# A sparse-mask mixture of experts on one core: the next batch's routing placed among a batch's last three tiles

## What is computed

```
adj  = side (column) * cond (row) * softmax(x, axis=-1) / 32 ; diagonal = -inf
mask = 1.0 at the 10240 largest of the 1024*1024 values, else 0.0
scores = softmax(mask @ G)                    # 8 experts; the two best per row, with weights w
y = sum over the two experts e of  w * ( silu(mask @ gate_e) * (mask @ up_e) ) @ down_e
      + w * (mask @ lora_A_e) @ lora_B_e      # inner width 128, lora rank 16
out = x + y
```

## Time and profile before

| | us |
|---|---|
| median of 3 runs (lowest, highest) | 833.69 (831.17, 837.47) |
| the profiled execution: its time | 836.23 |
| its span | 834.5 |
| first layers begin: batch 0, 1, 2, 3 | 165.7, 328.7, 502.7, 676.7 |
| tile 20's first layer begins: batch 0, 1, 2 | 279.6, 454.0, 626.3 |

### The profile page before, as it was taken

The page is one execution under the profiler, slowest core; times in us unless marked ns, Lnnn a source line. Parts: engine busy times, 40 slices in busy tenths (PEclk is TensorE's granted clock), DMA queues, the critical chain, the costliest instruction groups (busy, mean ns, idle before and its releaser), DMA issues.

```text
span 834.5 us, 14610 instructions
## 1 busy us (share of the span) xinstructions
PE 529.9 (63%) x4178; PEld 358.9 (43%) x4178; DVE 519.5 (62%) x1242; ACT 455.4 (55%) x655; POOL 388.8 (47%) x337
## 2 busy tenths in 40 slices
PE   0211376289888754787887726987788368798810
PEld 0200365156555533454555414654455146465500
DVE  5768799576778465865885676757861623233335
ACT  6686387658744564485444553874445345355510
POOL 7123200234473114487786124877871157767510
PEclk9755599589999995898899967999999869899965
DMA  9980340114232904478377734685678247767569
GB/s 315 358 234 0 115 189 26 45 55 158 88 127 86 356 28 129 147 252 288 107 263 240 319 104 148 215 287 174 212 247 334 77 131 252 268 212 264 203 234 380
DMA packets 80443, 159.93 MB, mean 192 GB/s; under 512 B 22889, under 2 KB 32105, under 8 KB 79856
## 3 DMA queue, kind: packets, MB, share of 16 engines
q1 hardware_dynamic: 59760, 108.60, 37.8%
q0 software_dynamic: 20608, 50.37, 17.3%
HBM read 107.53 MB, written 73.40 MB: 217 GB/s over the span
## 4 chain that ended last, share of the span: by engine, by line
DMA 19%; PE 18%; DVE 17%; issue 15%; POOL 14%; ACT 8%; DVEq 4%; SPq 3%; POOLq 1%; ACTq 0%
DMA out_dram<-piece 7%; DMA piece<-put_rows 6%; PE pa L676 5%; ACT mask L791 3%; DMA xg<-mask_rows,where 3%; POOL piece L526 3%; POOL piece L529 3%; DVE mask L1060 3%; DVE w L1166 2%; PE pb L663 2%; POOL xg L509 2%; ACT t_row L828 2%; DMA w<-put_rows 2%; PE pd L625 2%; POOL put_rows L517 2%
## 5 line engine op out<-in xcount | busy, mean ns | idle before, releaser
L676 PE MATMUL pa<-w,xt 128*128 x1472 | 203.2, 294 | 1.1 <-issue 0.9
L848 ACT ACTIVATE y<-pc,where 128x512 f32<-128x512 f32 x184 | 125.3, 687 | 104.8 <-PE pc L702 97.4
L676 PEld LDWEIGHTS pa<-w,xt 128*128 128x128 f16 x1472 | 150.7, 103 | 62.1 <-issue 14.7
L517 POOL DMA_INDIRECT put_rows<-y,where x92 | 92.5, 1005 | 151.9 <-ACT y L848 133.3
L1336 DVE SCALAR_TENSOR_TENSOR g_full<-pa,where,s_act 128x144 f32<-128x144 f32 x92 | 33.5, 365 | 197.0 <-ACT s_act L840 196.9
L509 POOL DMA_INDIRECT xg<-mask_rows,where x92 | 97.4, 1058 | 122.8 <-DVEq L1328 92.9
L835 ACT ACTIVATE xt<-pb 128x1024 f16<-128x1024 f16 x92 | 94.3, 1025 | 101.7 <-PE pb L663 98.7
L663 PE MATMUL pb<-ident,xg 128*128 128x128 f16 x736 | 61.4, 231 | 68.5 <-DMA xg<-mask_rows,where 46.2
L663 PEld LDWEIGHTS pb<-ident,xg 128*128 128x128 f16 x736 | 48.7, 104 | 80.1 <-DMA xg<-mask_rows,where 53.5
L840 ACT ACTIVATE s_act<-pa,small 128x128 f32<-128x128 f32 x92 | 33.8, 368 | 86.8 <-PE pa L676 86.8
L702 PE MATMUL pc<-lb,gt 128*128 x184 | 77.4, 420 | 0.0
(11 more groups left out here) (208 smaller groups left out, 880.0 us busy)
## 6 DMA issues: line engine op xcount, KB each, us to landing
piece<-put_rows SPq DMA_DIRECT2D x96, 256.0 KB
v<-in_x_dram SPq DMA_DIRECT2D x40, 512.0 KB, 9.1
piece<-in_x_dram SPq DMA_DIRECT2D x48, 256.0 KB
out_dram<-piece SPq DMA_DIRECT2D x48, 256.0 KB, 3.8
mask_rows<-mask SPq DMA_DIRECT2D x4, 2048.0 KB, 16.6
w<-put_rows SPq DMA_DIRECT2D x16, 512.0 KB, 10.2
w<-in_L_ffn_gate_w_dram SPq DMA_DIRECT2D x8, 512.0 KB, 10.2
w<-in_L_ffn_up_w_dram SPq DMA_DIRECT2D x8, 512.0 KB, 8.3
```

The lines of the kernel that those rows point to most:

```text
L517: pool.indirect_dma_start(out=put_rows[n % 2], out_offset=bass.IndirectOffsetOnAxis(ap=put_row[n][:, i:i + 1], axis=0), in_=y[:, g % NY, : ...
L676: last = pe.matmul(l1[g % 2], xt[:, g % 2, t, :], w1[:, bass.ds(e, 1), t, k, :].rearrange("p o n -> p (o n)"), start=(t == 0 and k == 0), ...
L848: nc.scalar.activation(y[:, g % NY, half * HALF:(half + 1) * HALF], pc[:, half, :], ACT.Copy, scale=y_scale[n][:, i:i + 1]).then_inc(y_rea ...
```

## The change

The tables get new places, and work that stood outside the loop over tiles gets places in it. The three counts, the search below the threshold, mask, check and turns come up to two tiles earlier, and the 8 turns of the mask lie in tiles 17 to 19 where they lay in 19 to 22. The last score comes in tile 20, `choose` in 20, `weigh` and `place_pairs` ahead of tile 21's gate, `fill_table` behind it, `take_slots` ahead of tile 22's gate; PE's `rank` and `place_slots` stand in tiles 20 and 22. Four exponentials of batch n+2 stand in tile 20 on ACT, the other four at the start of batch n+1 between `store_xt(n, 1)` and the first `silu`. Of the eight maxima two stand in tile 19, two in 20 and four in tile 22, behind `take_slots`. On POOL the three first gathers of the next batch stand between the put of tile 20 and those of tiles 21 and 22. On SP `move_mask` stands two pieces earlier, and pieces 12 to 15 are added one tile later (17 to 20).

```diff
--- before.py
+++ after.py
@@ -76,29 +76,36 @@
     SCALE_AT = {(0, 0): 0, (0, 1): 1, (0, 2): 2, (1, 0): 3, (1, 1): 4, (1, 2): 5, (2, 0): 6, (2, 1): 7}
     SIDE_SUM_AT = (1, 3)
     DIAG_AT = 3
-    AIM_AT = {(2, 2): 1, (5, 1): 2, (8, 0): 3, (10, 1): 4}
+    AIM_AT = {(2, 2): 1, (5, 1): 2, (7, 2): 3, (9, 2): 4}
     DVE_COUNT_AT = {(3, 1): (1, 0), (3, 2): (1, 1), (4, 0): (1, 2), (5, 2): (2, 0), (6, 0): (2, 1),
-                    (6, 1): (2, 2), (8, 0): (3, 0), (8, 1): (3, 1), (8, 2): (3, 2)}
+                    (6, 1): (2, 2), (7, 2): (3, 0), (8, 0): (3, 1), (8, 1): (3, 2)}
     ACT_COUNT_AT = {(3, 0): (1, 0), (3, 1): (1, 1), (3, 2): (1, 2), (4, 0): (1, 3), (5, 2): (2, 0),
-                    (6, 0): (2, 1), (6, 1): (2, 2), (6, 2): (2, 3), (8, 1): (3, 0), (8, 2): (3, 1),
-                    (9, 0): (3, 2), (9, 1): (3, 3)}
-    SUM_AT = {(5, 0): 1, (7, 2): 2, (10, 0): 3}
-    BELOW_AT = {10: (0, 2), 11: (4,), 12: (6, 7)}
-    DVE_BELOW_AT = {(10, 1): 1, (11, 1): 3, (12, 1): 5}
-    BEST_AT = {(10, 2): 0, (11, 0): 1, (11, 2): 2, (12, 0): 3, (12, 2): 4, (13, 0): 5, (13, 1): 6, (13, 2): 7}
-    NEAREST_AT, NEAREST_SPREAD_AT = (14, 1), (14, 3)
-    RANK_AT = {(15, 0): (0, 1), (15, 1): (2, 3)}
-    PICK_AT, PICK_SUM_AT = (15, 2), (16, 0)
-    MASK_AT = {(16, 1): (0, 1), (16, 2): (2, 3), (17, 0): (4, 5), (17, 1): (6, 7)}
-    MASK_SUM_AT = (18, 1)
-    CHECK_AT = (18, 2)
-    TURN_AT = {(19, 0): 0, (19, 2): 1, (20, 0): 2, (20, 2): 3, (21, 0): 4, (21, 2): 5, (22, 0): 6, (22, 2): 7}
-    STORE_MT_AT = dict(TURN_AT)
-    MAX_AT = {(19, 2): 0, (20, 0): 1, (20, 1): 2, (20, 2): 3, (21, 0): 4, (21, 2): 5, (22, 0): 6, (22, 2): 7}
-
-
-    PIECE_AT = {**{j + 1: j for j in range(9)}, **{j + 4: j for j in range(9, PIECES)}}
-    PIECES_FIRST = 14
+                    (6, 0): (2, 1), (6, 1): (2, 2), (6, 2): (2, 3), (8, 0): (3, 0), (8, 1): (3, 1),
+                    (8, 2): (3, 2), (9, 0): (3, 3)}
+    SUM_AT = {(5, 0): 1, (7, 1): 2, (9, 2): 3}
+    BELOW_AT = {10: (0, 2), 11: (4, 6), 12: (7,)}
+    DVE_BELOW_AT = {(10, 0): 1, (11, 0): 3, (12, 0): 5}
+    BEST_AT = {(10, 1): 0, (10, 2): 1, (11, 0): 2, (11, 1): 3, (11, 2): 4, (12, 0): 5, (12, 1): 6, (12, 2): 7}
+    NEAREST_AT, NEAREST_SPREAD_AT = (13, 0), (13, 2)
+    RANK_AT = {(14, 0): (0, 1), (14, 1): (2, 3)}
+    PICK_AT, PICK_SUM_AT = (14, 2), (15, 0)
+    MASK_AT = {(15, 1): (0, 1), (15, 2): (2, 3), (16, 0): (4, 5), (16, 1): (6, 7)}
+    MASK_SUM_AT = (16, 3)
+    CHECK_AT = (17, 0)
+    TURN_AT = {(17, 1): 0, (17, 3): 1, (18, 0): 2, (18, 2): 3, (18, 3): 4, (19, 0): 5, (19, 2): 6, (19, 3): 7}
+    STORE_MT_AT = {(17, 1): 0, (17, 2): 1, (18, 0): 2, (18, 1): 3, (18, 2): 4, (19, 0): 5, (19, 1): 6, (19, 2): 7}
+    LAST_SCORE_AT = (20, 1)
+
+    CHOOSE_AT, WEIGH_AT, PLACE_AT, TABLE_AT, SLOTS_TAKEN_AT = (20, 1), (21, 0), (21, 0), (21, 1), (22, 0)
+    PAIR_RANK_AT, SLOTS_AT = (20, 3), (22, 0)
+    PROBS_AT = (20, 2)
+
+    MAX_AT = {(19, 1): (0,), (19, 2): (1,), (20, 0): (2,), (20, 2): (3,), (22, 1): (4, 5), (22, 2): (6, 7)}
+    EXPS_FIRST = 4
+
+
+    PIECE_AT = {**{j + 1: j for j in range(9)}, **{j + 4: j for j in range(9, 12)}, **{j + 5: j for j in range(12, PIECES)}}
+    PIECES_FIRST = 12
 
     with ExitStack() as ctx:
         def sb(name, shape, dt):
@@ -529,11 +536,15 @@
                 nc.gpsimd.tensor_tensor(piece[:, at, 0, :], piece[:, at, 0, :], piece[:, at, 2, :],
                                         ALU.add).then_inc(summed_piece, 1)
 
-            for n in range(B):
+            def first_gathers(n):
                 pool.wait_ge(routed, n + 1)
                 pool.wait_ge(mask_stored, 16 * (n + 1))
                 for i in range(NX):
                     gather(n, i)
+
+            for n in range(B):
+                if n == 0:
+                    first_gathers(0)
                 if n >= 2:
 
                     pool.wait_ge(summed_piece, PIECES * (n - 1))
@@ -549,8 +560,11 @@
                             below_third(n + 1, q)
                     if n > 0 and i in PIECE_AT:
                         sum_piece(n - 1, PIECE_AT[i])
-                for i in range(T - 3, T):
-                    put_out(n, i)
+                put_out(n, T - 3)
+                if n + 1 < B:
+                    first_gathers(n + 1)
+                put_out(n, T - 2)
+                put_out(n, T - 1)
 
         @block.tensor
         def _(pe):
@@ -751,6 +765,12 @@
                         turn_mask(n + 1, c)
                         if c > 0:
                             score(n + 1, c - 1)
+                    if (i, spot) == LAST_SCORE_AT:
+                        score(n + 1, C - 1)
+                    if (i, spot) == PAIR_RANK_AT:
+                        rank(n + 1)
+                    if (i, spot) == SLOTS_AT:
+                        place_slots(n + 1)
 
                 for i in range(T):
                     experts[i] = load_expert(n, i)
@@ -765,15 +785,9 @@
                     if i >= 2:
                         second_layer(n, i - 2, experts[i - 2])
                     between(i, 3)
-                if more:
-                    score(n + 1, C - 1)
                 turn_g(n, T - 1)
                 second_layer(n, T - 2, experts[T - 2])
-                if more:
-                    rank(n + 1)
                 second_layer(n, T - 1, experts[T - 1])
-                if more:
-                    place_slots(n + 1)
 
         @block.scalar
         def _(act):
@@ -898,9 +912,17 @@
                         count(n + 1, k, p)
                     if more and (i, spot) in STORE_MT_AT:
                         store_mt(n + 1, STORE_MT_AT[i, spot])
+                    if more and (i, spot) == PROBS_AT:
+                        probabilities(n + 1)
+                        if n + 2 < B:
+                            for c in range(EXPS_FIRST):
+                                exponential(n + 2, c)
 
                 store_xt(n, 0)
                 store_xt(n, 1)
+                if n > 0 and more:
+                    for c in range(EXPS_FIRST, C):
+                        exponential(n + 1, c)
                 for i in range(T):
                     silu(n, i)
                     if i + 2 < T:
@@ -914,13 +936,8 @@
                     between(i, 2)
                 store_y(n, T - 2, 0)
                 store_y(n, T - 2, 1)
-                if more:
-                    probabilities(n + 1)
                 store_y(n, T - 1, 0)
                 store_y(n, T - 1, 1)
-                if n + 2 < B:
-                    for c in range(C):
-                        exponential(n + 2, c)
 
         @block.vector
         def _(dve):
@@ -1420,8 +1437,19 @@
                         make_mask(n + 1, MASK_AT[here])
                     if here == CHECK_AT:
                         check_mask(n + 1)
+                    if here == CHOOSE_AT:
+                        choose(n + 1)
+                    if here == WEIGH_AT:
+                        weigh(n + 1)
+                    if here == PLACE_AT:
+                        place_pairs(n + 1)
+                    if here == TABLE_AT:
+                        fill_table(n + 1)
+                    if here == SLOTS_TAKEN_AT:
+                        take_slots(n + 1)
                     if n + 2 < B and here in MAX_AT:
-                        maximum(n + 2, MAX_AT[here])
+                        for c in MAX_AT[here]:
+                            maximum(n + 2, c)
 
                 for i in range(T):
                     between(i, 0)
@@ -1431,8 +1459,6 @@
                         store_gt(n, i - 1)
                     between(i, 2)
                 store_gt(n, T - 1)
-                if more:
-                    route(n + 1)
 
 
             for c in range(C):
```

## The result

| | before | after |
|---|---|---|
| median, us (lowest, highest; 4 runs each, taken together) | 832.76 (831.17, 837.47) | 868.11 (865.51, 869.08) |
| span of the profiled execution | 834.5 | 865.5 |
| first layers begin: batch 0, 1, 2, 3 | 165.7, 328.7, 502.7, 676.7 | 165.3, 337.8, 522.9, 709.2 |
| tile 20's first layer: batch 0, 1, 2 | 279.6, 454.0, 626.3 | 301.2, 485.4, 673.6 |

The change makes the kernel slower: ratio 1.041, 95% interval [1.036, 1.046]. The prediction said 840 us with a range of 818 to 856: the measured time lies 28 us above the first and 12 above the end of the range.

A forecast was written before the change was run, and what follows sets the result against it. Waits, not engine shares, were taken to bound the kernel. Batches 0 to 3 summed -1.4, +4.9, +0.9 and +2 to +6.4 us, added to 833.7: forecast 840 us, range 818 to 856.

The forecast's parts named there:

- Step 1: Search, mask and turns two tiles earlier: tile 20's first layer later by net +9.7, +11.0, +10.2 us in batches 0 to 2.
- so 3.1: Between first and last `take_best`, DVE does two gates and two copies less, so the pick comes 3.1 us earlier.
- waits 4.1 us more: PE's wait for the mask's counts at the end of tile 16; tile 17 starts 12.9 us after the pick's sum.
- 12.9 + 24.9 = 37.8: Tile 17's start plus tiles 17 to 19 with turns: tile 20 comes 37.8 us after the pick's sum, before 23.7.
- Step 2: Routing inside tiles 20 to 22: tile 20 to next first layer shortens by 11.1, 10.7 and 13.9 us in batches 0 to 2.
- Step 3: Four exponentials at the batch's start delay the first silu: +4.6 us in batches 1 and 2; those in tile 20 free.
- Step 4: Pieces and the DMA burst of `x` and mask: no cost in batches 1 and 2, +2 us in batch 3.
- (a): Overlap pays: tile 16's wait costs nothing, second layer of tile 20 at full clock, no piece late: 821 us; chance 0.28.
- (b): Burst lands 6 us later, delaying POOL's puts and the mask's copy, 8 us in each of two batches: 856; chance 0.20.
- (c): Each table switch also drains ScalarE: four new switches in batches 1 and 2 add 5.1 us: 845; chance 0.07.
- the sign of the forecast: Whole kernel slower by +6.4 us; chances faster 0.30, same 0.33, slower 0.37.

The follow-up runs named there:

- w1: Kernel before with only the third count, its sums and aims in their new places: 844.70 us, ratio 1.012.
- w2: w1 with the products below the threshold and the nearest value in their new places too: 855.72 us, ratio 1.025.
- z2: Kernel before without the two low-part products of each half of a second layer: 816.59 us, ratio 0.985.
- x4: Changed kernel with GpSimd's product for the seventh row block moved back from tile 11 to tile 12: 888.93 us, ratio 1.061.
- x5: Kernel before with counts, search, mask, its sum and check in their new places, turns left in tiles 19 to 22: 863.28 us, ratio 1.040.
- x1: Kernel before with only the new places of search, mask and turns; routing, exponentials, pieces and gathers as before: 872.19 us, ratio 1.042.
- y1: Changed kernel with the second four exponentials at the end of tile 22 instead of the next batch's start: 866.10 us, ratio 1.038.
- y2: Changed kernel with pieces 12 to 15 and the mask's copy in their old places: 869.34 us, ratio 1.040.

## Why the prediction was wrong, by its steps

**Step 1 failed: "+11.0", "+9.7" and "+10.2".** Measured: 22.0 in batch 0, and, after taking off what the exponentials cost (below), 19.1 and 24.2 in batches 1 and 2. It failed in three terms: how soon the pick comes, the wait at tile 16, and the three tiles with the turns. Their rows, TensorE's sums of the pick and of the counts in all three batches:

```profile
257.61 0.38 PE L576 MATMUL pm<-small,ones 128*128 128x1 f32 x2 [0.18 <-DVE small L1069]
...
441.82 0.38 PE L576 MATMUL pm<-small,ones 128*128 128x1 f32 x2 [0.74 <-DVE small L1069]
456.14 0.59 PE L576 MATMUL pm<-small,ones 128*128 128x1 f32 x2 [6.72 <-DVE small L1081]
457.02 3.52 PE L690 MATMUL pa<-w,xt 128*128 x16 [0.29 <-issue]
...
628.57 0.38 PE L576 MATMUL pm<-small,ones 128*128 128x1 f32 x2 [0.73 <-DVE small L1069]
642.88 0.59 PE L576 MATMUL pm<-small,ones 128*128 128x1 f32 x2 [6.71 <-DVE small L1081]
```

- *"The pick comes earlier in time ... so 3.1."* It came later: in batch 0 at 257.61, 254.58 before. Counted from the first layer and without the exponentials' share it is +3.4 (92.3 against 88.9), -0.8 (104.0 against 101.6, less 3.2) and +3.7 (105.7 against 99.1, less 2.9). So 2.3 to 6.8 us are missing here. The 3.1 was misread to begin with: between the first and the last `take_best` the trace has three gates and three copies before, two and three after, so one gate less (1.2 us) and no copy. And even that was not won, since the stretch takes 18.6 us, before 16.5, 19.4 and 16.5. The tightening ahead of it I took as free, where w1 and w2 show what it can cost: 1.2%, and 2.5% with the search below the threshold.
- *"PE gets there at about 8.4 and waits 4.1 us more; tile 17 starts at 12.9."* The waits were 5.7, 6.7 and 6.7, and tile 17 started 13.9, 15.2 and about 15.2 after the pick's sum.
- *"12.9 + 24.9 = 37.8."* Tiles 17 to 19 took 29.7, 28.4 and 29.8, where 6.3, 9.4 and 9.2 had been summed: tile 17 began on the lower clock and took 8 to 9, each of the other two 10 to 11 us. Tile 20 came 43.6, 43.6 and 45.0 after the pick's sum.

Underneath lies one error of view. I asked of each wait what it adds to the tiles, and of the search how much sooner it would be. The traces say that the search keeps about its duration whether 19, 18 or 17 tiles run beside it: from the first silu to the mask's end it is 98 to 105 us in batch 0 and 106 to 115 in the others in all kernels but z2 (96, 105, 107: lighter tiles) and w2 and x4 (up to 110 and 118). Placing it in fewer tiles decides mainly how few tiles run beside it. What fixes the duration from within, beyond the stretch of `take_best` named above, was not taken apart. The sum should have had the tiles and turns behind the mask as its main term: from the mask's end to tile 20's first layer it took 30.9, 29.5 and 31.0 us, before 12.4, 11.4 and 11.7. That is 18 to 19 of the 22 to 27 us. x5 gives 6.5 to 11 of it to the two tiles; the rest goes with the turns that now stand ahead of tile 20, and comes back behind it.

**Step 2 was right in number, but most of its gain is not early routing.** Forecast 38.0, 38.0 and 36.3 from tile 20 to the next first layer, measured 36.6, 37.5 and 35.6. Its pieces in the trace, GpSimd at the end of batch 0:

```profile
329.07 0.98 POOL L524 DMA_INDIRECT put_rows<-y,where  x1 [11.72 <-ACT y L862]
330.35 1.06 POOL L516 DMA_INDIRECT xg<-mask_rows,where  x1 [0.30 <-issue]
```

The put of tile 20 came 27.9 after its first layer (28.2 forecast), the first gather 29.2 (29.5). The step gains 11 to 15 us, and only gives back part of what step 1 loses. x1, which has no early routing, already takes only 39.7, 39.3 and 39.6 us for the same stretch: the turns moved ahead of tile 20 give 9 to 11 us, the early routing and the rest 2 to 4 more. In x1 the tiles behind the mask run down to the routing in 4 us each (silus of tiles 21 and 22 at 310.2 and 313.9 in batch 0); in the changed kernel they are stretched over it.

**Step 3 was right in place, a little high.** ScalarE, batch 1, between the second copy and the first silu:

```profile
338.64 1.28 ACT L796 ACT_TABLE_LOAD   x1
...
344.38 0.18 ACT L796 ACTIVATION_READ_ACCUMULATOR v<-v,small 128x1 f32 x1
344.58 1.28 ACT L854 ACT_TABLE_LOAD   x1
345.88 0.37 ACT L854 ACTIVATE s_act<-pa,small 128x128 f32<-128x128 f32 x1
```

Silu 0 comes 8.1 us after the first layer (337.8), 8.5 forecast. Of the 4.6 us, 3.2 and 2.9 were left at silu 3, and y1 puts the whole at 2 us (868.1 less 866.1), with intervals that overlap.

**Step 4 had the wrong sign, by little**: batch 3 was 1.5 us shorter from its first layer, +2 forecast. y2 cannot tell the pieces' new places from nothing.

**The rivals.** (a) did not happen: tile 20 came 22 us late, not less than 5. (b) did not, though it came near: GpSimd waited 8.1 and 7.2 us for piece 14 in batches 1 and 2, about the 8 us that the prediction had set as the limit, and the boundaries behind it were as short as forecast. `choose` waited for no copy. Its rows in batches 1 and 2, where the burst is, have no bracket:

```profile
489.15 0.35 DVE L1234 TENSOR_REDUCE mask<-pm 128x64 f32<-128x192 f32 x1
...
677.38 0.35 DVE L1234 TENSOR_REDUCE mask<-pm 128x64 f32<-128x192 f32 x1
```

(c) is excluded: 20 ns lie between the last read (344.56) and the table load, and 20 ns between its end and silu; the load ahead of the exponentials starts 20 ns behind the copy before it as well (338.62 and 338.64). The Trainium skill, "ScalarE: Activation LUTs", "What ACT_TABLE_LOAD costs", counts 1.38 us of drain for each switch; by that, as an estimate, silu 0 would have come near 11 us after the first layer. This trace does not show it, and the measurement decides. My chances gave "slower" 0.37, but for reasons that were not the one, so it is luck that the sign of the forecast agrees with the result. The case that came true, a search that takes its own time, was not among the rivals.
